# Sorting two of four pairs of token chunks by expert, with GpSimd moving rows only

## The reference

```
t = tokens(x)                                   # 8192 tokens of 64 channels
logits = norm(t) @ gate_w + gate_b
top, index = top_k(logits, 2); w = softmax over the two
# layers 0 and 3: 16 experts, hidden 128
out_e = (silu(norm(t) @ w1[e]) * (norm(t) @ w2[e])) @ w3[e]
# layers 1 and 2: 8 experts, hidden 256
out_e = gelu(norm(t) @ W1[e] + b1[e]) @ W2[e] + b2[e]
t = t + sum over the two chosen experts of w_e * out_e
```

## Time and profile before

| | us |
|---|---|
| median of 3 runs | 1995.5 (1994.68 to 1995.93) |
| the profiled execution | 2001.35 |
| its span | 1999.6 |
| PE busy | 1647.4 (82%) |
| DVE busy | 1232.4 (62%) |
| ACT busy | 907.4 (45%) |
| POOL busy | 790.8 (40%) |

### The profile page before, as it was taken

One profiled execution on the slowest core, in us unless ns is written; L12 is line 12 of the kernel. 1 busy time (PEld: TensorE's weight loads), 2 busy tenths in 40 slices (PEclk: granted clock), 3 DMA queues, 4 the chain that ended last, 5 costly groups with the idle time before them and its releaser, 6 DMA issues. The chain is left out here.

```text
span 1999.6 us, 32592 instructions
## 1 busy us (share of the span) xinstructions
PE 1647.4 (82%) x11943; PEld 940.0 (47%) x11943; DVE 1232.4 (62%) x1822; ACT 907.4 (45%) x1451; POOL 790.8 (40%) x693
## 2 busy tenths in 40 slices
PE   6857887787877999987999978999997567777887
PEld 3624443443424454444444446777775333334343
DVE  6678773566787443466543456566664787744676
ACT  3433433343405555534646526666664433333342
POOL 3315871486312605111604234233330158623773
PEclk8879998998988999998999998999999789998899
DMA  5017884587601433211343230000000168864886
GB/s 156 1 47 139 185 186 135 119 173 161 151 3 33 142 105 90 63 37 25 106 138 89 75 72 1 1 2 2 2 1 3 31 133 197 164 156 107 173 176 119
DMA packets 118424, 184.75 MB, mean 92 GB/s; under 512 B 28244, under 2 KB 45588, under 8 KB 117620
## 3 DMA queue, kind: packets, MB, share of 16 engines
q1 hardware_dynamic: 106036, 159.52, 35.5%
q0 software_dynamic: 12224, 23.09, 3.7%
HBM read 165.63 MB, written 16.91 MB: 91 GB/s over the span
## 5 line engine op out<-in xcount | busy, mean ns | idle before, releaser
L1026 PE MATMUL ps<-tokens_high,w_high 64*128 64x512 f32 x1152 | 264.2, 454 | 163.6 <-DVE mx_hidden L1211 146.2
L1287 POOL TENSOR_TENSOR mx_hidden<-mx_hidden,mx_gates 128x512 f32<-128x512 f32 x192 | 285.2, 1493 | 194.1 <-DMA mx_gates<-gate_board 107.0
L1176 ACT ACTIVATE mx_hidden<-ps 128x1024 f32<-128x1024 f32 x192 | 196.4, 1025 | 228.6 <-PE ps L1109 210.2
L1222 DVE TENSOR_TENSOR mx_hidden<-mx_hidden,mx_gates 128x512 f32<-128x512 f32 x192 | 191.6, 998 | 145.3 <-DMA mx_gates<-gate_board 106.9
L1026 PEld LDWEIGHTS ps<-tokens_high,w_high 64*128 64x128 f32 x1152 | 113.6, 193 | 318.5 <-DVE mx_hidden L1211 229.4
L2465 DVE TENSOR_TENSOR c_near_weights<-c_near_hats 128x768 f32<-128x768 f32 x192 | 190.1, 1037 | 103.1 <-PE ps L2336 103.0
L1420 ACT ACTIVATE mx_hidden<-ps,w_bias 128x1024 f32<-128x1024 f32 x192 | 199.1, 1116 | 104.5 <-PE ps L1026 104.4
L1026 PE MATMUL ps<-tokens_low,w_high 64*128 64x512 f32 x1152 | 236.3, 405 | 0.0
L1026 PE MATMUL ps<-tokens_high,w_low 64*128 64x512 f32 x1152 | 235.9, 404 | 0.0
L1109 PE MATMUL ps<-mx_hidden,w_second 128*64 128x512 f32 x768 | 203.7, 652 | 5.5 <-DVE x L1227 4.0
L1211 DVE TENSOR_TENSOR mx_hidden<-ps,mx_hidden 128x1024 f32<-128x1024 f32 x192 | 183.7, 957 | 30.6 <-PE ps L1026 23.0
(11 more groups left out here) (279 smaller groups left out, 2321.8 us busy)
## 6 DMA issues: line engine op xcount, KB each, us to landing
mx_gates<-gate_board SPq DMA_DIRECT2D x192, 512.0 KB
mx_gates<-gate_board SPq DMA_DIRECT2D x192, 128.0 KB
mx_by_tokens<-sorted_board POOLq DMA_DIRECT2D x14, 512.0 KB, 10.5
out_board<-mx_by_tokens POOLq DMA_DIRECT2D x14, 512.0 KB, 3.3
w_first<-in_f_first SPq DMA_DIRECT2D x4, 1024.0 KB, 11.8
mx_by_first<-in_f_first_of SPq DMA_DIRECT2D x64, 64.0 KB, 3.8
mx_by_second<-in_f_second_of SPq DMA_DIRECT2D x48, 65.0 KB, 2.6
mx_by_first<-in_f_first_of SPq DMA_DIRECT2D x48, 64.2 KB, 2.5
```

Of the source, the lines that this page charges most:

```text
L1026: last = pe.matmul(out[h], weights[w][half(h), w_own], tokens[t][half(h), t_own], start=(p == 0), stop=(p == 2))
L1176: act.activation(hidden[:, n % HIDDEN], first[:, n % FIRST], ACT.Silu).then_inc(s.act.semaphore, 1)
L1222: dve.tensor_tensor(own, own, gates.spread[:, n % gates.SLOTS, 0, :], ALU.mult).then_inc(s.gated.semaphore, 1)
L1287: pool.tensor_tensor(own, own, gates.spread[:, n % gates.SLOTS, 1, :], ALU.mult).then_inc(s.gated_other.semaphore, 1)
```

## The change

- Both mixtures are built with `sorted_pairs=2`: four dense chunks (64 and 32 steps), 32 sorted tiles, four units, 24 and 20 turns of the phase, 64 scatters and 64 gathers a mixture. The boards get 96 instead of 64 slots, so six transfers instead of four clear them at the start.
- In SwiGLU DVE multiplies both halves by the gates in one instruction; POOL does nothing but the remaining low parts of tokens, scatters, load, store and gathers, one after the other.
- The SwiGLU board of gates lies by chunk, expert, half, column: a step reads one piece of 4 KB for each partition instead of two of 2 KB.
- The router's choice for the sorted pairs is done for both pairs at once (instructions of twice the elements).
- The order: `AFTER` goes from 48 to 32 (SwiGLU) and from 24 to 22 (GELU), units are laid at steps 0 to 3, and merged at 45, 51, 57 and the end (SwiGLU), or all four behind the last step and the next norm's first four chunks (GELU). The next norm waits for the merges before its fifth chunk.

```diff
-SWIGLU = Mixture(experts=16, hidden=128, sorted_pairs=1)
-GELU = Mixture(experts=8, hidden=256, sorted_pairs=1)
+SWIGLU = Mixture(experts=16, hidden=128, sorted_pairs=2)
+GELU = Mixture(experts=8, hidden=256, sorted_pairs=2)
...
             def means(n):
+                if turn > 0 and not router:
+                    k.mx.merged.wait(pe, 0)
...
-            rows = self.board.rearrange("(h e) c -> e h c", h=HALVES)[e, :, chunk(i)]
-            sp.dma_start(self.spread[:, n % self.SLOTS, :, :], rows.partition_broadcast(P)).then_inc(
-                self.s.gate[n % self.SLOTS].semaphore, 16)
+            sp.dma_start(self.spread[:, n % self.SLOTS, :, :].rearrange("p h c -> p (h c)"),
+                         self.by_expert[i, e].rearrange("h c -> (h c)").partition_broadcast(P)).then_inc(
+                             self.s.gate[n % self.SLOTS].semaphore, 16)
...
     def gather(self, pool, i):
...
+        if unit >= 2 and i % 16 == 0:
+            self.arrived(pool, unit - 2)
...
 def mixture_swiglu(k, ctx, w, layer, tokens, top_two, following):
...
-    AFTER = 3 * E
+    AFTER = 2 * E
...
-    LAY_AT, MERGE_AT = (1, 3), (85, 91)
-    SQUASH_AT = {11: 1, 37: 2, 61: SORTED}
-    SCATTER_AT, GATHER_AT, EACH = 6, AFTER + 2, 2
+    LAY_AT, MERGE_AT = (0, 1, 2, 3), (45, 51, 57, STEPS - 1)
+    SQUASH_AT = {13: 1, 37: SORTED}
...
         def gate(n):
             s.act.wait(dve, n + 1)
             gates.wait(dve, n)
-            own = hidden[:, n % HIDDEN, 0, :]
-            dve.tensor_tensor(own, own, gates.spread[:, n % gates.SLOTS, 0, :], ALU.mult).then_inc(s.gated.semaphore, 1)
+            own = hidden[:, n % HIDDEN]
+            dve.tensor_tensor(own, own, gates.spread[:, n % gates.SLOTS], ALU.mult).then_inc(s.gated.semaphore, 1)
...
     @block.gpsimd
     def _(pool):
-        def gate(n):
-            s.act.wait(pool, n + 1)
-            gates.wait(pool, n)
-            own = hidden[:, n % HIDDEN, 1, :]
-            pool.tensor_tensor(own, own, gates.spread[:, n % gates.SLOTS, 1, :], ALU.mult).then_inc(
-                s.gated_other.semaphore, 1)
...
         pool.wait_ge(k.gt.gates, top_two.done(0))
-        token_low(k, pool, tokens, EARLY)
-        gate(0)
-        for n in range(0, STEPS, 2):
-            gate(n + 1)
...
+        for i in range(EARLY, DENSE):
+            token_low(k, pool, tokens, i)
+        pool.wait_ge(k.gt.low, lows(k, DENSE - 1))
+        for i in range(2 * by.NT):
+            by.scatter(pool, i)
+        by.load(pool)
+        by.store(pool)
+        for i in range(2 * by.NT):
+            by.gather(pool, i)
...
 def mixture_gelu(k, ctx, w, layer, tokens, top_two, following):
...
-    AFTER = 24
+    AFTER = 22
...
-    LAY_AT, MERGE_AT = (0, 1), (43, 46)
-    SQUASH_AT = {8: 1, 18: 2, 34: SORTED}
+    LAY_AT, MERGE_AT = (0, 1, 2, 3), (STEPS - 1,) * 4
+    SQUASH_AT = {8: 1, 26: SORTED}
...
         following.head_tensor(pe, ready)
+        for unit in range(by.UNITS):
+            out.free(pe, "merge", unit)
+            by.merge(pe, unit, out.bank("merge", unit))
```

## The result

The changed kernel took **1985.85 us** (median of 5 runs, 1980.88 to 1987.37) against 1995.93 of before in the same rounds: ratio 0.9941, 95% interval 0.9924 to 0.9958. With 11 more runs of it beside 16 of before on one chip (last part of the experiments) the ratio was 0.9916, 0.9891 to 0.9942. So it is faster by 0.6 to 0.8%, 12 to 17 us, where 20 had been forecast. The profiled execution of after has a span of 1981.2 us (1983.03 as timed), before had 1999.6.

The account below looks back on a forecast made before the run. SwiGLU steps were taken as paced by gate transfers, GpSimd and collisions with VectorE, GELU's dense steps by PE. SwiGLU -132 and GELU +112 gave -20 from the median 1995.5, so 1976 us, range 1940 to 2030.

Parts of the forecast that it names:

- SwiGLU ahead of the phase, -40: Each SwiGLU mixture up to its sorted phase: the phase starts at 277 instead of 317 us, -40.
- The phase, +31: SwiGLU's sorted phase: eight more turns at SyncE's 3.9 us a turn, +31 us a mixture.
- SwiGLU behind the phase, -57: From SwiGLU's phase to the norm's fifth chunk: 107 us instead of 164, -57 a mixture, gathers hidden.
- The gates in 4 KB pieces, 2.6 us a step between bounds of 2.0 and 3.1: SwiGLU dense steps: gate transfers put at 2.6 us a step, 2.8 where VectorE's limit is felt too.
- GELU, +54 and 2 for the clock: Each GELU mixture: GpSimd's serial chain puts the norm 54 us later, plus clock restarts; +112 for both mixtures.
- the term for the clock: GELU: PE restarts at a granted clock of 0.50, estimated 1 us on each of four restarts.
- The lock: SwiGLU moves: GpSimd and VectorE can fall into step; bounds 1.26 and about 1.8 us a move, 1.45 taken.
- the slower rival: SwiGLU: GpSimd and VectorE fall into step, a move costs 1.75 us; +66 for two mixtures, 2042 us; chance 0.25.
- the rival without a hold: SwiGLU: a move costs 1.26 us beside any VectorE work; -24 in all, 1952 us; chance 0.07.
- The sum, -20: Whole kernel: SwiGLU -132 and GELU +112 give -20 us, subtracted from the runs' median of 1995.5.

Follow-up runs that it names:

- e8: Changed kernel with the second layer's weight loads left out from the phase's seventh turn on, two loads a turn instead of four: 1913.90 us, ratio 0.9561.
- e2: Kernel before, one sorted pair everywhere, with only the new gate board and VectorE gating both halves: 1936.28 us, ratio 0.9676.
- e3: Changed kernel with the gate board as before, so gates arrive in two 2 KB pieces instead of one of 4 KB: 2017.47 us, ratio 1.0077.
- e10: e2 with the next chunk's gates transposed behind step 5 instead of 9 and posted behind the issue for step 12 instead of 13: 1876.98 us, ratio 0.9394.
- e6: Changed kernel with every second row move left out in GELU, 32 scatters and 32 gathers a mixture instead of 64 each: 1862.51 us, ratio 0.9303.
- e4: Changed kernel with GELU's sorted phase behind 28 dense steps instead of 22: 1986.28 us, ratio 0.9914.
- e7: Changed kernel with SwiGLU's gate product cut to 8 columns of each half instead of 512, gates still fetched: 1948.66 us, ratio 0.9750.
- e1: Changed kernel with the GELU mixtures put back to one sorted pair and their old order, SwiGLU as changed: 1863.07 us, ratio 0.9317.
- e12: e1 with earlier gates (1859.30 us), changed so SyncE reads both experts' numbers before a turn's four weight loads: 1852.57 us, ratio 0.9273.

## Why the prediction was right, point by point

- **SwiGLU ahead of the phase, -40:** right. From the mixture's first activation to the phase's took 190.3 us before and 149.8 after, -40.5 (layer 3: -44.3). The first scatter came 3.4 us later than forecast, and the scatters went at 1.41 in place of 1.45, 3 us less for the 64. They set the start of the phase: the last dense activation ends 16 us ahead of the last scatter (251.2 against 267.2).
- **The phase, +31:** right, +31.9 in both, and e8 shows that it is SyncE.
- **SwiGLU behind the phase, -57:** right in size, -56.5 and -58.9, but by luck: pieces were off in opposite directions. I put 2.8 us on a step; a pair takes 5.2, which is 2.6. I put 6 us on the change of chunk and some 2.3 on each merge; ACT in after shows one of each:

```profile
387.73 1.02 ACT L1189 ACTIVATE mx_hidden<-ps 128x1024 f32<-128x1024 f32 x1 [1.45 <-PE ps L1120]
...
392.95 1.02 ACT L1189 ACTIVATE mx_hidden<-ps 128x1024 f32<-128x1024 f32 x1 [1.29 <-PE ps L1120]
396.44 1.02 ACT L1189 ACTIVATE mx_hidden<-ps 128x1024 f32<-128x1024 f32 x1
404.38 1.02 ACT L1189 ACTIVATE mx_hidden<-ps 128x1024 f32<-128x1024 f32 x1 [6.92 <-PE ps L1120]
410.02 1.03 ACT L1189 ACTIVATE mx_hidden<-ps 128x1024 f32<-128x1024 f32 x1
```

  From 392.95 to 410.02 are three steps in 17.1 us where 7.8 would do, 9.3 for a change of chunk and a merge. Steps, change and three merges together took some 96 us (358.20 to 451.93 and one step more) where the sum had 103. The term that was too small is the last: 4 us from the last step to the norm's fifth chunk. From the last activation (451.93) to that square (469.89) it is 18.0 us, for the norm's first four chunks and the last merge stand there; before it was 13.3. So the stretch took 112 us and not 107, but the 164 that it was taken from end at the fourth chunk, 2.4 us early, and the step from the phase to the first dense activation became 1.8 us shorter. In e2 no such slips cancelled: the steady pair was right, the stops between chunks were not in my expectation, and it was wrong by 66 us.
- **The gates in 4 KB pieces, 2.6 us a step between bounds of 2.0 and 3.1:** the direction is shown by e3, and in after the transfers are no longer the bound (share 0.55 in steady steps; in e10 no step waits for gates at 2.7 us a step), so the true figure lies below VectorE's 2.6. It entered the sum as the 0.2 us by which a step was put at 2.8, 6 us a mixture, and they aren't there.
- **GELU, +54 and 2 for the clock:** right, +57.8 and +56.2. Its steps, from the mixture's first activation: first scatter at 34.4 us (forecast 31.8), a scatter 1.313 (1.31 on average), the phase's first transpose at 124.2 (122.8), first gather at 199.5 (196.3), last gather's end at 283.4 (278.3), fifth chunk at 292.0 (285.8 without the clock). The chain ends 6.2 us late. 2.6 of it arose at the first scatter: the sort put VectorE's first step off by 2.4 us, under the 3 that I had added for it, but from there to the first scatter it was 15.6 us in place of 4.8, where I had put 6.7 more. 1.9 is for gathers at 1.317 in place of 1.28, and 2.8 is the clock; other steps gave about 1 us back. PE in before at its last merge, to be laid beside the row at 843.44 above:

```profile
847.67 2.02 PE L963 MATMUL ps<-identity,mx_by_tokens 128*128 128x128 f32 x16 [0.74 <-DVE mx_by_tokens L955]
```

  The same 16 transposes take 3.75 us in after at a granted clock of 0.50 (843 to 847 us) and 2.02 in before at 1.00: PE had stood for 16.89 us ahead of them. At the start of the phase, after 31 us of standing, the way from the first transpose to the first activation is 3.3 us in place of 2.2. Together that is 2.8 us in the chain (2.6 in layer 2), where the prediction had 2. Of the 6.2 us 2.4 don't show in the difference, because the fourth chunk was taken for the fifth in before, and the term for the clock covers 2 more. e6 shows that the chain bounds, e4 that the length of the holes costs nothing. The 3.35 us of a GELU step don't follow from the windows named beside them (93 us for 24 steps, sort included, is 3.9), but in after two steps take 6.66 us (ACT, 631.24 to 637.90), which is 3.33.
- **The lock:** the slower rival needed 1.57 us a move, 1.41 was measured, and never near 1.75. GpSimd and VectorE do not fall into step. But a hold there is: e7 prices the gate product's share of it at 0.12 us a move on average. That speaks against the rival without a hold. By the Trainium skill ("SBUF — State Buffer", section "Who interferes with whom") such a product takes only the read interface, and issuing a DMA, by inference, is not held: here a scatter that starts during one takes 1.29 us on average where it takes 0.97 alone. Whether what is held is the reading of a move's 128 row numbers from SBUF or the writing of its descriptors no run separates; only the second would contradict that inference.
- **The sum, -20:** -22.4 in the mixtures, -18.3 in the span, -12 to -22 in the runs. It is the difference of two terms that were each right to some 3%, +114 (forecast 112) and -136 (132); an error of 15% in one of them would have hidden or turned the sign. The measured medians lie 8 to 10 us above 1976. I had subtracted from the median a difference worked out on a single profile, which was 5 us above its median; how much of the 8 to 10 us is that scatter stays open.

The step that I left out is not in the sum but in the choice: nothing in it says that the two halves of the change should be judged apart. The table gives -136 us for one and +114 for the other, and e1 takes the first alone.

## What to carry to other kernels

Price a change separately for every stage with its own limit, and ask of each whether it could be made without the others: here two mixtures, one paced by gates and GpSimd and the other by PE, answered the same edit with opposite signs. Work taken from PE is worth nothing where a serial chain of another engine grows by more; count that chain to its end, and look for what stands second before promising its whole length. And read a loop's cost over its seams as well as in its steady part: moving one small transpose four steps earlier, and its post to the board one, was worth 56 to 59 us, nearly as much as the new board and the new division of work together (65).

## What was not expected of the hardware

- The same 177 to 178 GB/s, broadcast gates for the most part, occupy the DMA engines at 0.55 in 4 KB pieces and at 0.95 in 2 KB pieces (after and e3).
- A row move issued by GpSimd takes 0.97 us alone. One that starts during VectorE's product of two SBUF operands (1.22 us) is held to the product's end and is over 0.8 to 0.9 us behind it, so it takes up to 1.97 us, 1.29 on average (after, the scatters of layer 0).
- Where gates come in 2 KB pieces, the last scatter took 7.17 us to land behind them, in place of 1.47 (e3 and after).
- SyncE reading a number from SBUF for an address costs nearly 0.6 us each time, one behind the other (e12), where issuing a load takes 0.67.
- How long PE mostly waits (granted clock 0.63 to 0.68 over such a stretch) costs nothing by itself (e4), but the first work behind the wait runs at a granted clock of 0.50: 16 transposes took 3.75 us in place of 2.02 (after and before).
